# The start of a Mamba and mixture-of-experts kernel: the first chunk in halves, with a queue of its own for the B and C rows

## The chip, the cores and the metric

The kernel runs on one core of one Trainium2 chip. The metric is the device time of one execution in microseconds; the time of a kernel is the median over its runs. Data are 32-bit floats. A core has TensorE (matrix products into PSUM), VectorE, ScalarE, GpSimd, and SP, which only issues transfers. ScalarE and GpSimd can issue transfers too.

## The reference, cut to what matters

The input x has 4 batches of 1024 tokens with 128 channels. Layer 0 is a selective state-space mixer (256 inner channels, 16 states) times the SiLU of a mixture of 8 experts; layer 1 is a linear attention times another mixture of experts. The change is in the front of layer 0's mixer:

```python
xn = layernorm(x)
xs, z = split(xn @ W_in)
xc = silu(causal_conv4(xs) + conv_b)
dbl = xc @ W_x                       # 64 columns for dt, 16 for B, 16 for C
dt = softplus(dbl[..., :64] @ W_dt + b_dt)
A = -exp(A_log)
h_t = exp(dt * A) * h_(t-1) + (dt * xc) * B_t      # a scan over t, for each of 16 states
y_t = sum over states of h_t * C_t
```

## The kernel before, in words

Channels lie on the 128 partitions, in two halves (`DK` = 2), tokens along the free axis. The sequence is cut into chunks of 512 tokens (`HALF`, eight chunks, `q`), so a batch has two. For each chunk and each of the 16 states there is one scan step, 144 in all, since the last chunk is done in two pieces. A step has: two decays on ScalarE (`pA`, L939), the product `dBx` = dtx times the B row on GpSimd (L738), two scans on VectorE (L1305), the product with the C row (`hc`, L1313), and eight transposes that sum over the states on TensorE (L829).

`make_plan` writes one list of stages, and each engine walks that list and takes its own part. So the order on each engine is fixed, and semaphores tie the engines together. The list begins with the front of chunk 0, one stage after the other: `xload`, `norm`, `xn`, `xT`, `xs`, `conv`, `thc`, `xc`, `dbl`, `dtr`, `soft`, `ln`, `dt`, `decay`. The scan steps follow, and between them stand the fronts of later chunks, the routing, the expert tiles and the sums ("extras").

The stages of the front, by lines of the kernel before. At the start VectorE clears `gy` (a tile of zeros), all PSUM banks, `xs`, `bd` and `bdw`, then waits for all small loads (`mix_loaded`), halves the convolution's weights `cw` and `cb`, and negates `am` after ScalarE has taken its Exp (L1146 to L1157). `norm`: mean and variance of eight tiles of 128 tokens on VectorE (L1167, L1170), eps and the power -1/2 on GpSimd (L681, L683). `xn`: eight normalising operations (L1182). `xT`, twice: four transposes (L765) and a copy (L963). `xs`, once per channel half: one projection (L804) and two ScalarE operations that read it, a copy (L1022) and the last tap of the convolution (L1024). `conv`: three taps per half on VectorE (L1267). `thc` and `xc`: SiLU as a Tanh (L1030) and one VectorE operation (L1277). `dbl`: the product with `W_x` (L810) and a copy (L1036). `dtr`: the product with `W_dt` (L817) and bias (L1048). `soft`, `ln`, `dt`: softplus as max(v, 0) + ln(1 + exp(-|v|)) with a correction of the rounding of 1 + e; Abs, Exp and Ln on ScalarE (L1053, L1055, L1059), then four VectorE operations (L1284 to L1287), and `dtx` = dt times xc (L1291).

The B and C rows of `dbl` go to device memory (`bc_rows`, L598, on SP's queue), and from there one row of B and one of C per step is spread over all partitions (`bcb`, three buffers, L951, on ScalarE's queue). At the start SP issues, in this order: x, the small loads (L584), six stores of zeros into the routed rows (L591), the weights of the experts (`exp_loads`, L594), six more stores of zeros, the store of the B and C rows, and the second batch of x (L581). The zeros are needed by the first scatter of tokens (L696), the experts' weights by their scaling on VectorE (L1329 to L1331), which stands behind the first scan step.

## Time and profile before

| | |
|---|---|
| time, median of 3 runs | 1222.59 us (1222.11 to 1223.76) |
| time of the profiled execution | 1228.98 us |
| its span | 1227.1 us |
| TensorE matmul busy | 919.4 us, 75% |
| VectorE busy | 967.1 us, 79% |
| ScalarE busy | 610.6 us, 50% |
| GpSimd busy | 594.1 us, 48% |
| mean granted TensorE clock | 0.874 of 2.4 GHz |

The span is the time from the first to the last event of the core in the profiled execution. Busy times are those in which the engine worked; they overlap one another. The page cuts the span into 40 equal slices of 30.7 us and gives each a digit. The timeline lists instructions in order of time; "x4" means that four are merged into a row, whose duration is then that of the group. What stands in brackets is the idle time before it and what ended it.

### The profile page before, as it was taken

To read this page: it belongs to the slowest core of one execution; us is meant where nothing else is said; L and a number is where in the kernel's file an instruction comes from. 1 tells how busy PE (TensorE), PEld (TensorE's weight loads), DVE (VectorE), ACT (ScalarE), POOL (GpSimd) and SP (SyncE) were. 2 spreads that over 40 slices of the span, in tenths; PEclk is the share of its full clock that TensorE was granted. 3 is DMA by queue.
4 is the path that set the end of the run, shared out by engine and by line. 5 is a ranking of instruction groups with operands and counts; after the bars stand their busy time and mean duration, and the time that the engine had idled before them with its cause. 6 is when DMAs were issued, how large, how long until landed. Compare 5 with 4: busy or idle time off the path is not lost.

```text
span 1227.1 us, 16938 instructions
## 1 busy us (share of the span) xinstructions
PE 919.4 (75%) x4540; PEld 650.9 (53%) x4540; DVE 967.1 (79%) x1808; ACT 610.6 (50%) x1585; POOL 594.1 (48%) x420
## 2 busy tenths in 40 slices
PE   2277587877677778876887889778676788889678
PEld 0054366545455555555655566556454565566456
DVE  4298689987998988877988797969658886888455
ACT  1343554563556545653665465645445554655233
POOL 0036523767436633785336333784774646335500
PEclk9676798896899988898998899988878897989888
DMA  8924334455434434553544534355644356445201
GB/s 263 284 73 105 101 86 98 136 141 140 120 104 112 110 85 108 141 139 117 121 95 115 123 97 112 108 159 133 152 115 113 79 117 167 103 110 133 66 5 31
DMA packets 168650, 144.71 MB, mean 118 GB/s; under 512 B 15680, under 2 KB 135536, under 8 KB 168560
## 3 DMA queue, kind: packets, MB, share of 16 engines
q10 hardware_dynamic: 39168, 67.12, 24.0%
q1 hardware_dynamic: 121712, 60.78, 17.4%
q0 software_dynamic: 7680, 15.74, 4.0%
q8 instruction: 41, 0.67, 0.2%
q14 instruction: 49, 0.40, 0.1%
HBM read 106.88 MB, written 36.70 MB: 117 GB/s over the span
## 4 chain that ended last, share of the span: by engine, by line
PE 30%; DVE 28%; issue 15%; POOL 11%; ACT 7%; SPq 4%; DMA 3%; another core or an unknown queue 1%; ACTq 1%; DVEq 0%; POOLq 0%
DVE pA L1305 10%; PE pM L919 5%; POOL dBx L738 5%; PE pH L829 3%; PE pM L909 3%; DVE hj L1341 3%; POOL rows_in L696 3%; PE p L884 3%; POOL gy L712 3%; PE pG L881 2%; PE pU L882 2%; SPq L594 2%; DVE hj L1353 2%; PE pG L884 1%; PE pH L897 1%
## 5 line engine op out<-in xcount | busy, mean ns | idle before, releaser
L738 POOL TENSOR_TENSOR dBx<-dtx,bcb 128x1024 f32<-128x1024 f32 (+1 forms) x144 | 305.7, 2123 | 453.7 <-DVE pA L1305 405.0
L829 PE MATMUL pH<-const,hc 128*128 128x128 f32 x1024 | 165.9, 310 | 55.2 <-DVE hc L1313 49.3
L1305 DVE TENSOR_TENSOR_SCAN pA<-pA,carry,dBx 128x512 f32<-128x512 f32 (+1 forms) x160 | 162.9, 1064 | 43.8 <-ACT pA L939 22.5
L939 ACT ACTIVATE pA<-dt,am 128x512 f32<-128x512 f32 (+1 forms) x288 | 173.9, 639 | 27.4 <-DVE hc L1313 19.0
L1305 DVE TENSOR_TENSOR_SCAN pA<-pA,dBx 128x512 f32<-128x512 f32 x128 | 149.8, 1216 | 38.7 <-POOL dBx L738 25.3
L829 PEld LDWEIGHTS pH<-const,hc 128*128 128x128 f32 x1024 | 131.2, 159 | 76.5 <-DVE hc L1313 57.4
L909 PE MATMUL pM<-const,hj 128*128 128x128 f32 (+3 forms) x636 | 131.5, 304 | 46.5 <-ACT hT L1114 13.3
L1313 DVE TENSOR_TENSOR hc<-pA,bcb 128x1024 f32<-128x1024 f32 (+1 forms) x144 | 159.3, 1106 | 5.0
L696 POOL DMA_INDIRECT rows_in<-xn,slots x120 | 127.4, 1062 | 30.4 <-issue 27.5
L909 PEld LDWEIGHTS pM<-const,hj 128*128 128x128 f32 (+3 forms) x636 | 74.2, 142 | 120.5 <-issue 82.2
L1111 ACT ACTIVATE yj<-pM 128x128 f32<-128x128 f32 x236 | 65.3, 277 | 137.7 <-PE pM L919 117.6
L1114 ACT ACTIVATE hT<-pM 128x256 f32<-128x256 f32 (+1 forms) x272 | 113.5, 417 | 34.8 <-PE pM L909 32.3
L881 PE MATMUL pG<-w13a,xgT 128*128 x184 | 84.1, 542 | 48.8 <-DVE hj L1353 46.7
L712 POOL DMA_INDIRECT gy<-rows_out,slots x96 | 94.9, 989 | 27.7 <-issue 24.4
L1341 DVE SCALAR_TENSOR_TENSOR hj<-tj,pG 128x352 f32<-128x352 f32 (+2 forms) x153 | 68.1, 445 | 47.0 <-ACT tj L1101 23.7
L919 PE MATMUL pM<-w2b,hT 128*128 (+1 forms) x448 | 99.4, 323 | 2.3 <-ACT hT L1114 1.5
L919 PEld LDWEIGHTS pM<-w2b,hT 128*128 128x128 f32 x448 | 73.6, 206 | 23.7 <-issue 8.0
L919 PE MATMUL pM<-w2a,hT 128*128 x552 | 81.5, 286 | 0.0
L882 PE MATMUL pU<-w13a,xgT 128*128 x184 | 79.3, 516 | 0.0
L919 PEld LDWEIGHTS pM<-w2a,hT 128*128 128x128 f32 x552 | 74.3, 204 | 0.2
L884 PE MATMUL p<-w13b,xgT 128*128 x108 | 50.6, 553 | 29.8 <-issue 15.2
L881 PEld LDWEIGHTS pG<-w13a,xgT 128*128 128x128 f32 x184 | 31.1, 207 | 69.0 <-issue 68.4
(205 smaller groups left out, 1536.2 us busy)
## 6 DMA issues: line engine op xcount, KB each, us to landing
bcb<-bc_rows ACTq DMA_DIRECT2D x112, 512.0 KB
rows_out<-yj SPq DMA_DIRECT2D x236, 64.0 KB
xg<-rows_in SPq DMA_DIRECT2D x176, 64.0 KB
bcb<-bc_rows ACTq DMA_DIRECT2D x32, 256.0 KB
rows_in<-gy SPq DMA_DIRECT2D x8, 512.0 KB, 5.6
mixed<-s_st SPq DMA_DIRECT2D x12, 256.0 KB, 2.4
so<-rows_out SPq DMA_DIRECT2D x6, 512.0 KB
sr<-mixed SPq DMA_DIRECT2D x6, 512.0 KB
```

The lines of the kernel that those rows point to most:

```text
L696: pool.indirect_dma_start(rows_in[l][b % 2], bass.IndirectOffsetOnAxis(ap=slots[l][b][:, c, k:k + 1], axis=0), xn[:, c, :], None).then_inc ...
L712: pool.indirect_dma_start(gy3[:, k, c, :] if b == LAST else gy[:, k, c, :], None, rows_out[l][b], bass.IndirectOffsetOnAxis(ap=slots[l][b] ...
L738: pool.tensor_tensor(dBx[:, N % 2, :, 0:t1 - t0], dtx[q % 2][:, :, t0:t1], row, ALU.mult).then_inc(dBx_ready, 1)
L829: last = mm(pH[:, half, c * DI + k * P:c * DI + (k + 1) * P], hc[:, N % 2, k, t * P:(t + 1) * P], ident, is_transpose=True, start=(n == 0 ...
L881: mm(pG[:, 0:hid], tok, w[:, 0:hid], start=True, stop=True).then_inc(gate_full, 1)
L909: last = pe.transpose(pM[0:w, m * P:(m + 1) * P], hj[i][:, k % 2, m * P:m * P + w], ident)
L919: last = mm(pM[:, YA:YA + P], hT[i][0:wd, m * P:(m + 1) * P], w[0:wd, m, :], start=(m == 0), stop=(m == len(ks) - 1))
L939: A(pA[:, k, 0:t1 - t0], dt[q % 2][:, k, t0:t1], ACT.Exp, scale=am[:, k, n:n + 1]).then_inc(decay_ready, 1)
L1114: last = A(hT[i][:, 0:w], pM[:, 0:w], ACT.Copy)
L1305: dve.tensor_tensor_scan(pA[:, k, 0:w], pA[:, k, 0:w], dBx[:, N % 2, k, 0:w], carry[:, k, N % NS:N % NS + 1] if N in carry_after else 0.0, ...
L1313: dve.tensor_tensor(hc[:, N % 2, :, 0:w], pA[:, :, 0:w], row, ALU.mult).then_inc(hc_ready, 1)
L1341: dve.scalar_tensor_tensor(out=hj[i][:, k % 2, 0:hid], in0=tj_of(i, k), scalar=1.0, in1=gate_bank(i, k)[:, 0:hid], op0=ALU.add, op1=ALU.mu ...
```

## The change

The list of stages of chunk 0 is new, and so is what they hold:

- The norm of batch 0 is done in halves of four tiles. Only the first half stands ahead of the projections; the second stands behind `xc`, and its transposes behind `dt`. Eps is now added on VectorE, for every front. GpSimd keeps the power, with its own tile of -1/2.
- VectorE clears one PSUM bank (`pM`) at the start and no other. The tile of zeros, `bd` and `bdw` are cleared on GpSimd.
- The waits are split: TensorE waits for `const` and `w_in`, VectorE for `cw` and `cb`, and all for the other small loads only at `dbl`, where the Exp of `am` now stands. `const`, `cw` and `cb` are loaded on ScalarE's queue.
- SP issues x, `w_in`, the other small loads, the experts' weights, and then all twelve stores of zeros.
- The convolution of a half follows its own projection; Tanh and, for chunk 0, `xc` are done by halves, and the product with `W_x` waits for each half by itself.
- For chunk 0 the store of the B and C rows is issued by ScalarE right behind the copy of `dbl`, and the first load of them behind Exp.
- Softplus: three VectorE operations stand at the stage `ln` and wait for Exp only; behind the logarithm one addition is left. This holds for all chunks.

```diff
@@ -217,9 +217,8 @@
-    plan = [("xload", 0), ("norm", 0, 0), ("xn", 0, 0), ("xT", 0, 0, 0), ("xs", 0, 0), ("xT", 0, 0, 1), ("xs", 0, 1),
-            ("conv", 0, 0), ("conv", 0, 1), ("thc", 0), ("xc", 0), ("dbl", 0), ("dtr", 0, 0), ("dtr", 0, 1),
-            ("soft", 0), ("ln", 0), ("dt", 0)]
+    plan = [("xload", 0), ("norm", 0, 0), ("xT", 0, 0, 0), ("xs", 0, 0), ("xs", 0, 1), ("conv", 0, 0), ("conv", 0, 1), ("thc", 0),
+            ("xc", 0), ("xn", 0, 0), ("dbl", 0), ("dtr", 0, 0), ("dtr", 0, 1), ("soft", 0), ("ln", 0), ("dt", 0), ("xT", 0, 0, 1)]
...
@@ -537,17 +538,21 @@
...
-            (const[:], T["const"]),
-            (w_in[:], T["L0_attn_W_in"]),
...
-            (cw[:], T["L0_attn_conv_w"].rearrange("(k p) j -> p k j", p=P)),
-            (cb[:], T["conv_b"]), (bdt[:], T["b_dt"]), (dpar[:], T["D_param"]),
...
+            (bdt[:], T["b_dt"]), (dpar[:], T["D_param"]),
...
@@ -580,8 +585,11 @@
+                        sp.dma_start(w_in[:], T["L0_attn_W_in"]).then_inc(w_in_loaded, 16)
...
+                        for dst, src in exp_loads:
+                            sp.dma_start(dst, src).then_inc(exp_loaded, 16)
...
-                            if l == 0:
-                                for dst, src in exp_loads:
-                                    sp.dma_start(dst, src).then_inc(exp_loaded, 16)
-                elif kind == "dbl":
+                elif kind == "dbl" and a[0]:
...
@@ -669,18 +674,23 @@
...
-                if kind == "norm":
+                if kind == "xload" and a[0] == 0:
+                    pool.memset(mhalf[:], -0.5).then_inc(mhalf_ready, 1)
+                    pool.memset(gy[:, 0], 0.0).then_inc(zero_tile, 1)
+                    pool.memset(bd[:], 0.0)
+                    pool.memset(bdw[:], 0.0).then_inc(zero_tile, 1)
+                elif kind == "norm" or (kind, *a) == ("xn", 0, 0):
...
-                        pool.wait_ge(mix_loaded, 16 * len(mix_loads))
...
-                    pool.wait_ge(stats_ready, F)
+                        c0, c1 = ((0, HT), (HT, CT))[kind == "xn"]
+                    no = F + (F > 1 or kind == "xn")
...
+                    pool.wait_ge(stats_ready, no)
...
-                    pool.tensor_scalar(vpe[:, cs], mv[:, cs, 1], EPS, None, ALU.add).then_inc(ve_ready, 1)
-                    pool.wait_ge(ve_ready, F)
-                    pool.tensor_tensor(rstd[:, cs], vpe[:, cs], mhalf[:, cs], ALU.pow).then_inc(rstd_ready, 1)
+                    pool.tensor_tensor(rstd[:, c0:c1], vpe[:, c0:c1], mhalf[:, c0:c1], ALU.pow).then_inc(rstd_ready, 1)
...
@@ -754,11 +764,15 @@
                 if kind == "xload" and a[0] == 0:
-                    pe.wait_ge(mix_loaded, 16 * len(mix_loads))
-                    pe.wait_ge(prepared, 1)
+                    pe.wait_ge(const_loaded, 16)
+                    pe.wait_ge(w_in_loaded, 16)
+                    pe.wait_ge(psum_cleared, 1)
                 elif kind == "xT":
...
-                    pe.wait_ge(xn_ready, front_no[l, b])
+                    if (l, b, m) == (0, 0, 0):
+                        pe.wait_ge(xn_first, 1)
+                    else:
+                        pe.wait_ge(xn_ready, front_no[l, b])
...
                 elif kind == "dbl":
...
-                    pe.wait_ge(xc_ready, q + 1)
+                    if q == 0:
+                        pe.wait_ge(mix_loaded, 16 * len(mix_loads))
...
+                        pe.wait_ge(xc_ready, DK * q + k + 1)
...
                 elif kind == "xs":
...
+                    act.wait_ge(conv_scaled, 1)
...
@@ -1024,16 +1039,23 @@
                 elif kind == "thc":
...
-                    act.wait_ge(conv_ready, 2 * (q + 1))
...
-                    A(v[:], ca[:], ACT.Tanh).then_inc(thc_ready, 1)
+                    for k in range(DK):
+                        act.wait_ge(conv_ready, DK * q + k + 1)
+                        A(v[:, k, :], ca[:, k, :], ACT.Tanh).then_inc(thc_ready, 1)
                 elif kind == "dbl":
...
+                    if q == 0:
+                        act.wait_ge(mix_loaded, 16 * len(mix_loads))
+                        A(am[:], am[:], ACT.Exp).then_inc(decay_exp, 1)
...
+                    if q == 0:
+                        act.wait_ge(bank_read, use["dbl", q])
+                        act.dma_start(bc_rows[0], dbl[R:R + 2 * NS, :]).then_inc(rows_stored, 16)
...
+                    if q == 0:
+                        bc_load(0)
...
                 elif kind == "decay":
-                    for N in range(BCR):
+                    for N in range(1, BCR):
...
-                    act.wait_ge(prepared, 2)
+                    act.wait_ge(decay_negated, 1)
...
@@ -1143,44 +1167,56 @@
...
-            dve.memset(gy[:, 0], 0.0).then_inc(zero_tile, 1)
-            for t in (pA, pH, pG, pU, p1, pM):
-                dve.memset(t[:], 0.0)
-            dve.memset(xs[:], 0.0)
-            dve.memset(bd[:], 0.0)
-            dve.memset(bdw[:], 0.0).then_inc(prepared, 1)
-            dve.wait_ge(mix_loaded, 16 * len(mix_loads))
-            dve.tensor_scalar(cw[:], cw[:], 0.5, None, ALU.mult)
-            dve.tensor_scalar(cb[:], cb[:], 0.5, None, ALU.mult)
-            dve.wait_ge(decay_exp, 1)
-            dve.tensor_scalar(am[:], am[:], -1.0, None, ALU.mult).then_inc(prepared, 1)
-            dve.wait_ge(prepared, 2)
+            def moments(src, c0, c1):
...
+                for c in range(c0, c1):
+                    last = dve.bn_stats(stats[:, c, :], src[:, c, :])
+                link(last)
+                for c in range(c0, c1):
+                    last = dve.bn_aggr(mv[:, c, :], stats[:, c, :])
+                link(last)
+                dve.tensor_scalar(vpe[:, c0:c1], mv[:, c0:c1, 1], EPS, None, ALU.add).then_inc(stats_ready, 1)
...
+            def normalise(src, c0, c1):
+                for c in range(c0, c1):
+                    last = dve.tensor_scalar(xn[:, c, :], src[:, c, :], mv[:, c, 0:1], rstd[:, c:c + 1], ALU.subtract, ALU.mult)
+                return last
...
+            dve.memset(pM[:], 0.0).then_inc(psum_cleared, 1)
...
                 if kind == "norm":
...
+                    if (l, b) == (0, 0):
+                        moments(src, 0, HT)
+                        dve.wait_ge(stats_ready, 1)
+                        dve.wait_ge(rstd_ready, 1)
+                        normalise(src, 0, HT).then_inc(xn_first, 1)
+                        dve.wait_ge(conv_loaded, 32)
+                        dve.tensor_scalar(cw[:], cw[:], 0.5, None, ALU.mult)
+                        dve.tensor_scalar(cb[:], cb[:], 0.5, None, ALU.mult).then_inc(conv_scaled, 1)
+                        dve.wait_ge(conv_scaled, 1)
+                    else:
+                        moments(src, *cols(l, b))
...
-                    dve.wait_ge(stats_ready, F)
-                    dve.wait_ge(rstd_ready, F)
...
+                    if (l, b) == (0, 0):
+                        moments(src, HT, CT)
+                        dve.wait_ge(stats_ready, 2)
+                        dve.wait_ge(rstd_ready, 2)
+                        normalise(src, HT, CT).then_inc(xn_ready, 1)
+                    else:
+                        dve.wait_ge(stats_ready, F + 1)
+                        dve.wait_ge(rstd_ready, F + 1)
+                        normalise(src, *cols(l, b)).then_inc(xn_ready, 1)
...
                 elif kind == "conv":
...
-                    dve.wait_ge(bank_read, use["xs", q, 1])
+                    dve.wait_ge(bank_read, use["xs", q, k])
...
                 elif kind == "xc":
...
-                    dve.wait_ge(thc_ready, q + 1)
...
-                    dve.scalar_tensor_tensor(out=xc[q % 2][:], in0=v[:], scalar=1.0, in1=ca[:], op0=ALU.add, op1=ALU.mult
-                                             ).then_inc(xc_ready, 1)
-                elif kind == "dt":
+                    if q:
+                        dve.wait_ge(thc_ready, DK * (q + 1))
+                        dve.scalar_tensor_tensor(out=xc[q % 2][:], in0=v[:], scalar=1.0, in1=ca[:], op0=ALU.add, op1=ALU.mult
+                                                 ).then_inc(xc_ready, DK)
+                    else:
+                        for k in range(DK):
+                            dve.wait_ge(thc_ready, k + 1)
+                            dve.scalar_tensor_tensor(out=xc[0][:, k, :], in0=v[:, k, :], scalar=1.0, in1=ca[:, k, :], op0=ALU.add, op1=ALU.mult
+                                                     ).then_inc(xc_ready, 1)
+                elif kind == "ln":
...
+                    if q == 0:
+                        dve.wait_ge(decay_exp, 1)
+                        dve.tensor_scalar(am[:], am[:], -1.0, None, ALU.mult).then_inc(decay_negated, 1)
...
-                    dve.wait_ge(ln_ready, q + 1)
+                    dve.wait_ge(act_chain, 2 * q + 2)
...
-                    link(dve.tensor_tensor(g, dt[q % 2][:], g, ALU.subtract))
-                    dve.scalar_tensor_tensor(out=dt[q % 2][:], in0=v[:], scalar=0.0, in1=g, op0=ALU.max, op1=ALU.add
-                                             ).then_inc(dt_ready, 1)
+                    link(dve.scalar_tensor_tensor(out=g, in0=v[:], scalar=0.0, in1=g, op0=ALU.max, op1=ALU.subtract))
+                elif kind == "dt":
...
+                    dve.wait_ge(ln_ready, q + 1)
+                    dve.tensor_tensor(dt[q % 2][:], dt[q % 2][:], xs[:, :, 0:HALF], ALU.add).then_inc(dt_ready, 1)
...
-                    dve.wait_ge(xc_ready, q + 1)
+                    dve.wait_ge(xc_ready, DK * (q + 1))
...
```

## Rows read from the trace of the kernel before

**Rows 1.** The page: clock and DMA share in 40 slices; shares of the chain by engine.
```profile
PEclk9676798896899988898998899988878897989888
DMA  8924334455434434553544534355644356445201
...
PE 30%; DVE 28%; issue 15%; POOL 11%; ACT 7%; SPq 4%; DMA 3%; another core or an unknown queue 1%; ACTq 1%; DVEq 0%; POOLq 0%
```

**Rows 2.** The chain, 0 to 90 us: start us, duration us, engine and line.
```profile
48.29 4.90 DMA bc_rows<-dbl
53.21 5.64 DMA bcb<-bc_rows
...
58.98 2.35 POOL dBx L738
61.35 2.36 DVE pA L1305 x2
```

**Rows 3.** Timeline of SP's queue: start us, duration us, then what is issued.
```profile
0.73 0.43 SPq L581 DMA_DIRECT2D x<-in_L_attn_x  x1
...
15.79 3.11 SPq L594 DMA_DIRECT2D w13s<-in_L_ffn_sw  x2
...
40.43 7.82 SPq L591 DMA_DIRECT2D rows_in<-gy  x6
...
48.29 1.56 SPq L598 DMA_DIRECT2D bc_rows<-dbl  x1
```

**Rows 4.** Timeline of the compute engines, from the norm to dbl.
```profile
9.83 0.17 DVE L1153 TENSOR_SCALAR cw<-cw 128x8 f32<-128x8 f32 x1 [2.15 <-DMA queryT<-in_queryT]
...
10.31 1.65 DVE L1167 BATCH_NORM_STATS2 stats<-x 128x6 f32<-128x128 f32 x8
...
13.15 1.68 POOL L683 TENSOR_TENSOR rstd<-vpe,const 128x8 f32<-128x8 f32 x1
14.93 2.14 DVE L1182 TENSOR_SCALAR xn<-x,mv,rstd 128x128 f32<-128x128 f32 x8 [2.30 <-POOL rstd L683]
...
17.22 1.09 PE L765 MATMUL pM<-const,xn 128*128 128x128 f32 x4 [17.22 <-DVE xn L1182]
...
19.06 2.08 PE L804 MATMUL pM<-xnT,w_in 128*128 128x512 f32 x2 [0.75 <-ACT xnT L963]
...
21.73 0.77 ACT L1024 ACTIVATE ca<-pM,cb,cw 128x512 f32<-128x512 f32 x1
...
24.42 2.07 PE L804 MATMUL pM<-xnT,w_in 128*128 128x512 f32 x2 [0.69 <-ACT xnT L963]
...
27.88 4.57 DVE L1267 SCALAR_TENSOR_TENSOR ca<-xs,cw,ca 128x512 f32<-128x512 f32 x6 [10.79 <-ACT ca L1024]
...
34.85 3.58 PE L810 MATMUL pM<-xc,w_x 128*96 128x512 f32 x4 [8.36 <-DVE xc L1277]
...
38.47 0.59 ACT L1036 ACTIVATE dbl<-pM 96x512 f32<-96x512 f32 x1 [4.93 <-PE pM L810]
```

**Rows 5.** Timeline of the compute engines, softplus.
```profile
45.74 1.28 ACT L1059 ACT_TABLE_LOAD   x1
...
48.12 0.69 DVE L1284 TENSOR_SCALAR xs<-ca 128x1024 f32<-128x1024 f32 x1 [13.32 <-ACT dt L1059]
...
52.62 1.22 DVE L1291 TENSOR_TENSOR dtx<-dt,xc 128x1024 f32<-128x1024 f32 x1
```

**Rows 6.** DMA issues of 0 to 80 us: KB each, median us to landing.
```profile
w2a<-in_L_ffn_w SPq DMA_DIRECT2D x2, 512.0 KB, 11.0
...
const<-in_const SPq DMA_DIRECT2D x1, 275.5 KB, 4.2
```

**Rows 7.** Line L683 in 900 to 1000 us: duration ns, starts, form.
```profile
L683 POOL TENSOR_TENSOR rstd<-vpe,const x1: 1050/1050/1050, 990.5 to 990.5; 128x4 f32<-128x4 f32 x1
```

**Rows 8.** Timeline of GpSimd from 100 us: the first scatter.
```profile
101.66 1.46 POOL L696 DMA_INDIRECT rows_in<-xn,slots  x1 [0.19 <-issue]
```

**Rows 9.** Busy time per engine, clock and DMA share, one stretch.
```profile
292.00:408.00 116.00, 85.65 (x448) 62.88 (x449) 104.16 (x176) 63.66 (x144) 58.82 (x34) 0.90 0.43 117
```

More of the change, by code:

```diff
@@ L364, in program @@
         queryT = sb("queryT", [P, P])
-        NCONST = 3 * P + NE + NE * CT + TILES + NE + NE * CT
+        NCONST = 3 * P + NE + NE * CT + TILES + NE * CT
         const = sb("const", [P, NCONST])
@@ L372, in program @@
         last_at = 3 * P + NE + NE * CT + TILES
-        mhalf = const[:, last_at:last_at + NE]
-        goes_on = const[:, last_at + NE:NCONST]
+        goes_on = const[:, last_at:NCONST]
         x = sb("x", [P, CT, P])
@@ L389, in program @@
         vpe = sb("vpe", [P, CT])
+        mhalf = sb("mhalf", [P, CT])
         rstd = sb("rstd", [P, CT])
@@ L538, in program, with bc_row @@
         out_rows = [[sem(f"out_rows{i}{s}") for s in range(YR)] for i in range(2)]
+        def bc_row(N):
+            q, t0, t1 = SEGS[N // NS]
+            n = N % NS
+            src = bc_rows[q].rearrange("(w n) t -> n w t", w=2)[n:n + 1, :, t0:t1]
+            return bcb[:, N % BCR, :, 0:t1 - t0], src.broadcast_to([P, 2, t1 - t0])
         block = ctx.enter_context(nc.Block())
         mix_loads = [
-            (const[:], T["const"]),
-            (w_in[:], T["L0_attn_W_in"]),
             (w_x[:], T["L0_attn_W_x"].rearrange("(k p) n -> p k n", p=P)),
@@ L941, in bc_load @@
             def bc_load(N):
-                q, t0, t1 = SEGS[N // NS]
-                n = N % NS
-                if n == 0:
-                    act.wait_ge(rows_stored, 16 * (q + 1))
+                if N % NS == 0:
+                    act.wait_ge(rows_stored, 16 * (SEGS[N // NS][0] + 1))
                 if N >= BCR:
@@ L949, in bc_load @@
                     act.wait_ge(hc_ready, N - BCR + 1)
-                src = bc_rows[q].rearrange("(w n) t -> n w t", w=2)[n:n + 1, :, t0:t1]
-                act.dma_start(bcb[:, N % BCR, :, 0:t1 - t0], src.broadcast_to([P, 2, t1 - t0])).then_inc(bc_loaded[N % BCR], 16)
+                act.dma_start(*bc_row(N)).then_inc(bc_loaded[N % BCR], 16)
             for kind, *a in plan:
                 if kind == "xload" and a[0] == 0:
-                    act.wait_ge(mix_loaded, 16 * len(mix_loads))
-                    A(am[:], am[:], ACT.Exp).then_inc(decay_exp, 1)
-                    act.wait_ge(prepared, 1)
+                    act.dma_start(const[:], T["const"]).then_inc(const_loaded, 16)
+                    act.dma_start(cw[:], T["L0_attn_conv_w"].rearrange("(k p) j -> p k j", p=P)).then_inc(conv_loaded, 16)
+                    act.dma_start(cb[:], T["conv_b"]).then_inc(conv_loaded, 16)
                 elif kind == "xT":
@@ L977, in _ @@
                     b, = a
+                    act.wait_ge(zero_tile, 2)
                     act.wait_ge(bank_full, use["gram", b])
@@ L1045, in _ @@
                     if k == 0:
-                        act.wait_ge(xc_ready, q + 1)
+                        act.wait_ge(xc_ready, DK * (q + 1))
                     act.wait_ge(bank_full, use["dtr", q, k])
@@ L1161, in _ @@
                     l, b = a
-                    F = front_no[l, b]
                     src = x if l == 0 or b >= LAST else xr
@@ L1165, in _ @@
                         dve.wait_ge(x_in, 16 * (b + 1))
-                    for c in range(*cols(l, b)):
-                        last = dve.bn_stats(stats[:, c, :], src[:, c, :])
-                    link(last)
-                    for c in range(*cols(l, b)):
-                        last = dve.bn_aggr(mv[:, c, :], stats[:, c, :])
-                    last.then_inc(stats_ready, 1)
+                    if (l, b) == (0, 0):
[9 more added lines that the diff above has]
+                        moments(src, *cols(l, b))
                 elif kind == "xn":
@@ L1180, in _ @@
                         dve.wait_ge(scattered[pl][pb % 2], 16 * TOPK * CT * (pb // 2 + 1))
-                    for c in range(*cols(l, b)):
-                        last = dve.tensor_scalar(xn[:, c, :], src[:, c, :], mv[:, c, 0:1], rstd[:, c:c + 1], ALU.subtract, ALU.mult)
-                    last.then_inc(xn_ready, 1)
+                    if (l, b) == (0, 0):
[7 more added lines that the diff above has]
+                        normalise(src, *cols(l, b)).then_inc(xn_ready, 1)
                 elif kind == "top":
@@ L1455 @@
         np.eye(P), np.triu(np.ones((P, P)), 1) - 1, np.ones((P, P)), row * np.arange(NE), row * np.tile(P * np.arange(CT), NE),
-        row * np.arange(TILES), row * np.full(NE, -0.5),
+        row * np.arange(TILES),
         row * np.tile(np.arange(CT) > 0, NE)], axis=1).astype(np.float32))
```

20 lines of the change are left out of this document (12 added, 8 removed).

## The prediction

> **What bounds the kernel now.** I read the page's chain first, then the timeline of the first 72 us engine by engine, then the chain of the same stretch, then the queue's landings. The page's chain is spread over TensorE, VectorE, issue and GpSimd, with no one engine behind it [rows 1]: 144 scan steps in a fixed order. Nothing of that order is changed by this edit except in small ways, so the question is where the first scan starts and whether all that follows moves with it. It starts at 61.35 us [rows 2].
>
> The chain of the start shows why. The first dBx on GpSimd (58.98) waits for the first row pair of B and C; that load waits for the store of the rows, and the store stands at 48.29 in SP's queue, though ScalarE had written dbl at 38.47 + 0.59 = 39.06 [rows 2, 4]. In between SP issues six zeroing stores (7.82 us for six, because the queue is full) and before them the expert weights, from 15.79 to 40.43 [rows 3]. So the store loses 9.2 us to its place. Compute was done earlier too: dtx ends at 52.62 + 1.22 = 53.84, and the dBx could start at 53.95 rather than 58.98 [rows 2, 5]. So removing the queue alone is worth 5.0 us; then the arithmetic chain from x is next.
>
> **The chain after the change, step by step.** Start: x. It is the first load of SP's queue, issued at 0.73 [rows 3]; const, queued behind it and issued at 1.22 (0.49 later), takes 4.2 us to land, so by 5.4 [rows 6]. x is earlier than that and is now alone at the head of its queue, but shares the engines with const on ScalarE's. I take 5.0, between 4.2 and 5.4. Before, the norm began at 10.31, because VectorE cleared all of PSUM and then waited for the last small load [rows 4]. VectorE now has one memset ahead of the norm.
>
> - moments: before, 2.84 us from 10.31 to the pow at 13.15, with eight columns and two GpSimd steps; I put 0.5 of it to hand-overs and halve the rest (1.15); eps is now a VectorE op, 0.17 as the small op on cw, plus 0.2 of hand-over: 1.5 [rows 4]. -> 6.5
> - pow: 1.68 for 8 columns, 1.05 for 4 in the one row of that width [rows 4, 7]. -> 7.55 (by half of 1.68 it would be 0.84)
> - four xn: half of 2.14, with both hand-overs 1.35. -> 8.9
> - transposes to x-projection: 17.22 to 19.06, 1.84. -> 10.75
> - first projection and its two ScalarE copies: 19.06 to 22.50, 3.44. -> 14.2. The transposes of the second half no longer stand between the two projections.
> - second projection: 0.14 of hand-over, then 24.42 to the first convolution at 27.88, 3.46. -> 17.8. The first channel half is convolved meanwhile (three ops, 2.29, from 14.2 to 16.5), hidden behind the second projection.
> - second channel half: three ops, half of 4.57. -> 20.1
> - half Tanh and half xc: the whole took 34.85 - 32.45 = 2.40; half of it with a fixed part is 1.35. -> 21.45
> - second half of dbl: half of 3.58 plus 0.05, then the 0.59 copy. The first half ran before. -> 24.0 [all rows 4]
>
> dbl is thus written at 24.0 instead of 39.06. From there to the end of Exp nothing is changed but ScalarE's issue of the store, which lies beside its wait for TensorE's dtr: the table load behind Exp began at 45.74, 6.68 after dbl, so Exp ends at 30.7 [rows 4, 5]. Then two branches. ScalarE: issue of the first B/C load (0.4), table load and Ln (45.74 to 48.12, 2.38): 33.5. VectorE: negated am 0.2, then the three ops in front of the logarithm. The four of before took 48.12 to 52.62, 4.50; without one of 1.25 that is 3.25: 34.2. One op of 1.25 for dt, 1.25 for dtx: 36.7. dBx starts at 36.8, takes 2.35, and the scan starts at **39.2** [rows 2, 5]. VectorE, not Ln, is the later branch by 0.7, so one operation behind the logarithm instead of four is worth 33.5 + 4.5 = 38.0 (start of dtx in the old order) less 35.45 = 2.5 us, not the whole of three ops.
>
> What ScalarE does between Ln and the first decay: the copy of xT and the first Exp (512 wide, at most 0.77 each, as the copy at 21.73), two DMA issues (0.43 each, as SP's first) and a table load (1.28), from 33.5: 37.2, still ahead of dBx's end by 2.0 [rows 3 to 5]. The second half of the norm (four columns) sits on VectorE between xc (21.5) and Exp (30.7), 9 us for some 4 us of work. These cost nothing; if that gap were gone they would cost 4.
>
> **The B and C rows.** Their store is issued at 24.1. In the trace it took 4.90 us in SP's full queue, and the load 5.64 [rows 2]. With those durations the store lands at 29.0, ahead of Exp's end, and the load (issued 30.8) at 36.4, ahead of dtx by 0.3. That is the thinnest margin of the change. The trace has no row of this pair against a backlog of weights. The nearest above are the weight loads themselves, w2a with 11.0 us [rows 6]; the nearest below are the 4.90 and 5.64. At 11.0 each the store lands at 35.1, and as ScalarE waits for it with the table load, Ln, the xT copy and all decays queued behind that wait, the load is issued at 35.2, lands at 46.2 and the scan starts at 48.7. I take a little over the lower end, since the long rows were queued behind 1.4 MB loads of their own queue and this pair is not: 1 us for it. First scan at 40.2, so **21.1 us** earlier.
>
> The page's DMA row stands at 8 and 9 tenths in the first two slices, 61 us [rows 1]; so the rows share full engines, and I weigh what a rule says. The Trainium skill (Trainium Kernel Development and Optimization, Key Constraints) states that DMAs of the SP, ACT and POOL queues share the same 16 engines and that issuing from several only saves the sequencer's issue time: it speaks against an own queue. By it alone the rows would keep waiting for bytes and the pair would cost as in the 11.0 case. The skill's DMA: Bandwidth & Descriptors (Queues, rings and completion order) says that each engine goes round between the queues packet by packet; by that the pair has a half share at least and the lower end holds. No row here decides between them; SP's 7.82 us for six issues shows only that the issue time itself is large.
>
> **What moves with the first scan.** Expert weights are now issued straight behind the small loads, at 6.5 instead of 15.79; the same 24.6 us [rows 3] put the last issue at 31 and its landing at 36 at the latest. Their scaling on VectorE stands behind the first scan (40 + 3.5), so it waits for nothing. Zeroing follows: it had landed by 53.2 before, when the store behind it had [rows 2], and the three B/C loads of 1.5 MB now run among it, so 55 to 58. Its only user, the first scatter on GpSimd, was at 101.66 [rows 8], 80.5 after the shift: 22 us to spare. The second load of x stays behind the zeroing and is wanted by the norm of scan step 10. The PSUM banks that are no longer cleared and the memsets on GpSimd, which has nothing else to do before the first pow, cost nothing. No other time of the start is tied to the clock on the wall, so I count the shift in full.
>
> **Later chunks.** Tanh in halves adds some 0.15 us of ScalarE, 7 times; eps adds a VectorE op of 0.17 and a hand-over in 9 fronts, about 2.5 us if all of it lay on the chain, and takes one GpSimd op from each. The softplus ops of a chunk stand in two scan steps instead of one, with the same op count. I put the sum at 0, between -2 and +2.5.
>
> **Sum.** The profiled execution has a span of 1227.1 and a time of 1228.98; with 21.1 less, a span of 1206.0. The median of the three runs is 1222.59, 6.4 below the profiled one. 1222.6 - 21.1 = **1201.5 us**. Ends of the main case: first scan at 38.4 (x at 4.2, the pair as before) and -2: 1197.6; first scan at 43 and +2.5: 1206.7.
>
> **Rivals.**
> 1. Main case, 1197 to 1208: 0.80.
> 2. The B/C pair is slowed by the weights (toward 11.0 each), ScalarE is held. First scan at 45 to 49: 1207 to 1211. For it: the engines are full. Against it: the pair is small beside them. 0.08. The Key Constraints rule of the Trainium skill named above would give this time.
> 3. The own queue gets nothing until SP's backlog is gone: store at 53, Ln and load behind it, first scan at 60 to 62. That is 1221 to 1223, the case in which the change doesn't do what it says. 0.03. Its mild form, only the queue's 5.0 us won and the arithmetic as late as before, gives 1217.6: 0.02.
> 4. Slower: TensorE's clock. The page's clock row reads low in slices 2 to 5 [rows 1]; a stretch of 116 us at 0.90 has 85.65 us of matmul [rows 9], which at the 1.2 GHz level would be 154, so 38 us more for 116. If the new rhythm of the start kept the clock at 1.2 GHz for 65 us longer, the gain of 21 would be gone; at 80 us the time is 1201.5 + 26.2 = 1227.7. Against it: order and density of the scan stage are the same. 0.04.
> 5. Better than 1197: the clock rises earlier, the projections (2.08 and 2.07 [rows 4]) shorten. 0.03.
>
> **How the numbers follow.** A measurement of this kernel can tell 0.2% (2.4 us) from no change. Faster: cases 1, 2, 5 and the mild 3, 0.93. Within: case 3, 0.03. Slower: case 4, 0.04. The range takes case 1 and the near part of 2: 1196 to 1209.
>
> **What would show it.** dbl's copy should end near 24, Exp near 30.7, the first dBx start near 37 released by VectorE's dtx (if a bcb DMA releases it, the pair is the later); the idle time before Ln shows whether the store held ScalarE; the first scan near 40; the first scatter near 81 and not waiting for the zeroing. From first scan to the end it should take 1165.7 us as before, within 3. The forecast is wrong if x lands later than 6, if pow of four columns costs 1.68, or if that last distance grows.

## The result, and the profile after

The changed kernel took 1193.0 us (median of four runs, 1188.3 to 1197.5) against 1222.4 before; the ratio is 0.9757, with a 95% interval of 0.9716 to 0.9798. That is 29 us less, where 21 were forecast, and outside the forecast range. The profiled execution has a span of 1186.5 us and a time of 1188.29.

The chain of the start, after the change (start us, duration us, engine and line):

```profile
0.72 4.96 DMA x<-in_L_attn_x
...
7.35 1.04 POOL rstd L693
8.50 1.13 DVE xn L1182 x4
...
11.53 2.09 PE pM L818 x2
...
18.54 0.76 DVE ca L1303
...
21.61 3.50 PE pM L826 x4
25.13 0.60 ACT dbl L1055
...
36.99 1.24 DVE dtx L1338
...
38.30 2.35 POOL dBx L748
40.67 2.36 DVE pA L1352 x2
```

SP has left the chain: before, it stood in it from x to the store of the rows [rows 2, 3]. The first scan starts at 40.67 instead of 61.35, 20.7 us earlier; 21.1 were forecast. The queues and what waits for them, from the timeline:

```profile
25.76 0.34 ACTq L1058 DMA_DIRECT2D bc_rows<-dbl  x1
...
28.25 25.81 SPq L599 DMA_DIRECT2D rows_in<-gy  x12
...
31.39 1.06 ACT L1077 ACTIVATE ca<-ca 128x1024 f32<-128x1024 f32 x1
31.40 0.39 ACTq L964 DMA_DIRECT2D bcb<-bc_rows  x1
...
38.30 2.34 POOL L748 TENSOR_TENSOR dBx<-dtx,bcb 128x1024 f32<-128x1024 f32 x1 [13.55 <-DVE dtx L1338]
```

The load of B and C rows is issued at 31.40, as soon as Exp has started, so the store had landed: ScalarE was not held. The dBx was released by dtx on VectorE, not by a transfer; in three other traces it was the transfer (experiment 3). GpSimd's first scatter comes 20.0 us earlier than before [rows 8], straight behind its own work, with no wait for the zeros:

```profile
81.69 1.44 POOL L706 DMA_INDIRECT rows_in<-xn,slots  x1 [0.18 <-issue]
```

So the first scan is where it was forecast, and the missing 8 us lie behind it: from the first scan to the end it took 1145.8 us, where the forecast wanted 1165.7 within 3. I measure the scan stage from the start of the first product with a C row to that of the last (143 steps): 1075.4 us before (63.7 to 1139.1), 1056.6 after. The profiled execution of before is itself 6.6 us over its median, and the one after 4.7 us under it, so these two traces overstate the difference. By the medians the gain is 29.4 us; less these 20.7, some 8.7 us lie behind the first scan. That is why the cause was looked for in groups of traces, below.

One place where the scan stage is shorter shows in VectorE's timeline. The changed kernel, softplus of chunk 5, from scan step 75 to step 77:

```profile
623.97 1.22 DVE L1360 TENSOR_TENSOR hc<-pA,bcb 128x1024 f32<-128x1024 f32 x1
625.12 0.75 DVE L1328 TENSOR_SCALAR xs<-ca 128x1024 f32<-128x1024 f32 x1
625.90 1.23 DVE L1329 SCALAR_TENSOR_TENSOR xs<-xs,ca 128x1024 f32<-128x1024 f32 x1
627.16 1.22 DVE L1330 SCALAR_TENSOR_TENSOR xs<-v,xs 128x1024 f32<-128x1024 f32 x1
...
631.66 1.23 DVE L1360 TENSOR_TENSOR hc<-pA,bcb 128x1024 f32<-128x1024 f32 x1
...
635.06 1.22 DVE L1335 TENSOR_TENSOR dt<-dt,xs 128x1024 f32<-128x1024 f32 x1
636.31 1.23 DVE L1338 TENSOR_TENSOR dtx<-dt,xc 128x1024 f32<-128x1024 f32 x1
...
640.48 1.23 DVE L1360 TENSOR_TENSOR hc<-pA,bcb 128x1024 f32<-128x1024 f32 x1
```

And the same two steps in the kernel of experiment 1 that has the old softplus behind the new front; by chance its step 75 starts at the same time:

```profile
623.97 1.23 DVE L1379 TENSOR_TENSOR hc<-pA,bcb 128x1024 f32<-128x1024 f32 x1
626.09 0.33 ACT L1131 ACTIVATE tj<-pG 128x192 f32<-128x192 f32 x1
626.45 0.35 DVE L1407 SCALAR_TENSOR_TENSOR hj<-tj,pG 128x192 f32<-128x192 f32 x1 [1.25 <-issue]
...
629.07 2.35 DVE L1371 TENSOR_TENSOR_SCAN pA<-pA,dBx 128x512 f32<-128x512 f32 x2 [1.88 <-ACT pA L957]
631.45 1.22 DVE L1379 TENSOR_TENSOR hc<-pA,bcb 128x1024 f32<-128x1024 f32 x1
...
634.85 0.88 DVE L1348 TENSOR_SCALAR xs<-ca 128x1024 f32<-128x1024 f32 x1
...
639.55 1.23 DVE L1357 TENSOR_TENSOR dtx<-dt,xc 128x1024 f32<-128x1024 f32 x1
...
643.72 1.23 DVE L1379 TENSOR_TENSOR hc<-pA,bcb 128x1024 f32<-128x1024 f32 x1
```

Old order: VectorE idles 1.25 + 1.88 = 3.1 us in the first step, while it waits for ScalarE: first, by the times, for `tj` of an expert tile (ready at 626.42), then for the decays. It then has four softplus operations and dtx in one lump of 5.9 us (634.85 to 640.78) in the second. New order: the three operations that need only Exp fill the idle time of the first step. It ends only 0.2 us later (631.66 against 631.45), and the second is 8.8 us long instead of 12.3. The operation count is the same. How much of that a chunk keeps depends on its other steps, as the table below shows.

### The profile page after: what moved, and what is told of

It reads as the page before. It is cut to its first block, busy times and chain, and to the rows that moved or that the text cites. A ratio compares the mean times of both kernels' runs of the same rounds, so it can differ in the third digit from the quotient of the medians.

```text
span 1186.5 us, 16957 instructions
## 1 busy us (share of the span) xinstructions
PE 902.7 (76%) x4540; PEld 640.1 (54%) x4540; DVE 965.7 (81%) x1811; ACT 612.4 (52%) x1593; POOL 594.9 (50%) x415
## 4 chain that ended last, share of the span: by engine, by line
DVE 32%; PE 28%; POOL 15%; issue 12%; ACT 7%; DMA 4%; ACTq 1%; SPq 0%; DVEq 0%; POOLq 0%
DVE pA L1352 11%; POOL dBx L748 6%; POOL gy L722 5%; PE pM L935 4%; DVE hj L1388 3%; PE pH L845 3%; POOL rows_in L706 3%; PE pM L925 3%; PE pG L897 2%; PE p L900 2%; PE pU L898 2%; DVE hj L1400 2%; DVE hc L1360 2%; PE pH L913 1%; PE pG L900 1%
## 5 line engine op out<-in xcount | busy, mean ns | idle before, releaser
L845 PE MATMUL pH<-const,hc 128*128 128x128 f32 x1024 | 162.3, 306 | 49.0 <-DVE hc L1360 45.0
L845 PEld LDWEIGHTS pH<-const,hc 128*128 128x128 f32 x1024 | 128.4, 157 | 68.5 <-DVE hc L1360 52.0
L925 PE MATMUL pM<-const,hj 128*128 128x128 f32 (+3 forms) x636 | 130.2, 302 | 44.5 <-DVE hj L1400 18.3
L706 POOL DMA_INDIRECT rows_in<-xn,slots x120 | 129.8, 1082 | 30.4 <-issue 27.4
L900 PE MATMUL p<-w13b,xgT 128*128 x108 | 48.7, 535 | 30.7 <-DVE hj L1400 30.0
## 6 DMA issues: line engine op xcount, KB each, us to landing
rows_in<-gy SPq DMA_DIRECT2D x8, 512.0 KB, 10.3
```

The costliest lines, as they stand in the source:

```text
L706: pool.indirect_dma_start(rows_in[l][b % 2], bass.IndirectOffsetOnAxis(ap=slots[l][b][:, c, k:k + 1], axis=0), xn[:, c, :], None).then_inc ...
L845: last = mm(pH[:, half, c * DI + k * P:c * DI + (k + 1) * P], hc[:, N % 2, k, t * P:(t + 1) * P], ident, is_transpose=True, start=(n == 0 ...
L925: last = pe.transpose(pM[0:w, m * P:(m + 1) * P], hj[i][:, k % 2, m * P:m * P + w], ident)
```

## The experiments

Times are given as the ratio to the kernel before, run on the same chip in the same group, with its 95% interval. On the chips of experiment 1 and of the last run the kernel before itself scattered from 1220 to 1244 us, so there the traces say more than the times.

**Experiment 1: the front alone, and the softplus alone.** The yardstick, unaltered:

> The changed kernel once more, unaltered, as the yardstick of this group. Its first scan stands at 40.7 us, 20.7 earlier than before, as forecast; its median was 29.4 us below the one before and its runs lay 9 us apart. If the scatter belongs to the kernel, the median comes out between 1189 and 1197 again and the runs lie 6 us or more apart. If the 29.4 was chance of that chip, it comes out near 1201.

Measured: 0.9777 [0.9715, 0.9838]. The median was 1204.2, above the 1189 to 1197 expected, on a chip where before had 1232.6; the ratio agrees with the first measurement. The scan stage was 1064.5 us long.

The front alone: eps, Tanh and softplus of later chunks as before.

```diff
+                        pool.tensor_scalar(vpe[:, c0:c1], mv[:, c0:c1, 1], EPS, None, ALU.add).then_inc(ve_ready, 1)
...
+                    if q:
+                        act.wait_ge(conv_ready, DK * (q + 1))
+                        A(v[:], ca[:], ACT.Tanh).then_inc(thc_ready, DK)
+                        continue
...
+                    if q:
+                        continue
...
+                    if q:
+                        link(dve.tensor_scalar(g, ca[:], 1.0, None, ALU.add))
+                        link(dve.scalar_tensor_tensor(out=g, in0=g, scalar=1.0, in1=ca[:], op0=ALU.subtract, op1=ALU.subtract))
+                        link(dve.tensor_tensor(g, dt[q % 2][:], g, ALU.subtract))
+                        dve.scalar_tensor_tensor(out=dt[q % 2][:], in0=v[:], scalar=0.0, in1=g, op0=ALU.max, op1=ALU.add
+                                                 ).then_inc(dt_ready, 1)
```

> The changed front of chunk 0, with all that acts in later chunks undone: softplus in the old order, Tanh in one piece and eps on GpSimd for every chunk and batch but the first. Theory S (the 8 us beyond the forecast come from what the change does to later chunks): 1201.5, all of 21 us and no more. Theory T (an earlier start alone changes the rhythm of the scan stage, and with it TensorE's clock and the waits): 1193, the same as the whole change.

Measured: 0.9845 [0.9785, 0.9905], 19 us of 1222, with the first scan at 41.23. Theory S had said 1201.5, a ratio of 0.983; theory T 0.976, outside the interval. The scan stage is 1071.2 us long, hardly shorter than before.

The softplus alone, on the kernel before:

```diff
-                elif kind == "dt":
+                elif kind == "ln":
                     q, = a
                     g = xs[:, :, 0:HALF]
-                    dve.wait_ge(ln_ready, q + 1)
+                    dve.wait_ge(act_chain, 2 * q + 2)
...
-                    link(dve.tensor_tensor(g, dt[q % 2][:], g, ALU.subtract))
-                    dve.scalar_tensor_tensor(out=dt[q % 2][:], in0=v[:], scalar=0.0, in1=g, op0=ALU.max, op1=ALU.add
-                                             ).then_inc(dt_ready, 1)
+                    link(dve.scalar_tensor_tensor(out=g, in0=v[:], scalar=0.0, in1=g, op0=ALU.max, op1=ALU.subtract))
+                elif kind == "dt":
+                    q, = a
+                    dve.wait_ge(ln_ready, q + 1)
+                    dve.tensor_tensor(dt[q % 2][:], dt[q % 2][:], xs[:, :, 0:HALF], ALU.add).then_inc(dt_ready, 1)
```

> The kernel before, with only the softplus split: three VectorE operations at the stage ln, one behind the logarithm, for all chunks. In the traces of before and after, the pair of scan steps that holds these stages gained 2.6, 0.1, 3.0, 1.1 and 1.3 us in five of the seven chunks. Theory S: 1222.4 less 6 to 9, so 1214 to 1216. Theory T: 1222 to 1223.

Measured: 0.9897 [0.9836, 0.9957], 12.6 us less, with the first scan at 60.64, only 0.7 earlier than before. That is more than theory S asked for (0.993 to 0.995, inside the interval) and speaks against T (1.000, outside). 0.9845 x 0.9897 = 0.974: front and softplus add up to the whole change (0.976).

**Experiment 2: undoing the split, delaying the start, and the queue both ways.**

> The changed kernel with softplus in the old order from the second chunk on; eps on VectorE and Tanh in halves stay. If the split of softplus is the cause of the gain in later chunks: the scan steps 10 to 14 of chunks 3, 5, 6 and 7 are again 1 to 3 us longer each, and the time is that of the run with the front alone, 0.984 to 0.985 of before. If eps or Tanh is the cause: it stays near 0.977.

The softplus part of the diff of the front alone, and no other:

```diff
+                    if q:
+                        continue
                     g = xs[:, :, 0:HALF]
                     dve.wait_ge(act_chain, 2 * q + 2)
...
+                        link(dve.tensor_tensor(g, dt[q % 2][:], g, ALU.subtract))
```

Measured: 0.9889 [0.9855, 0.9923]; 0.984 to 0.985 was expected. Step 76 takes 12.3 us again, as before (8.8 with the split). The stretches with the softplus of chunks 3, 5, 6 and 7 are 0.7, 2.9, 0.9 and 4.1 us longer than in the first trace of the changed kernel. Not every long step is a loss: in chunk 4's stretch step 60 takes 15.5 us again instead of 10.6, but the step before it takes 6.0 instead of 7.9 and the two behind it 17.0 instead of 20.0, so the whole stretch changes by less than 0.1. The scan stage is 1071.1 us long, as with the front alone: the gain of the later chunks is gone with the split. The time is 5 us over the front alone, and the intervals overlap.

> The whole change, with VectorE held back by 20 chained memsets of an unused buffer behind the arrival of x, some 20 us, so that the first scan stands near 61 us as before. Theory S (front and later chunks add): 1222.4 - 8 = 1214, ratio 0.993 to 0.994. Theory T (an earlier start alone brings the later gain): 1222, ratio 1.000.

```diff
             dve.memset(pM[:], 0.0).then_inc(psum_cleared, 1)
+            dve.wait_ge(x_in, 16)
+            for _ in range(20):
+                link(dve.memset(xc[1][:], 0.0))
```

Measured: 0.9942 [0.9915, 0.9970]. The first scan came at 64.00, 2.7 us later than before, and still the time is 7.1 us less (theory S: 0.993 to 0.994). So the later gain needs no early start: theory T is out.

> The kernel before, with only this changed for chunk 0: ScalarE issues the store of the B and C rows behind the copy of dbl (near 39.1 us), and the first load of them behind Exp (near 45). By the sum of the forecast dtx is then next: first dBx at 53.95 instead of 58.98, first scan 5.0 us earlier at 56.3, time 1217.4. If weights and zeros in the other queue slow the pair to 11 us each, the first load lands at 61 or later and nothing is won.

```diff
-                elif kind == "dbl":
+                elif kind == "dbl" and a[0]:
...
+                    if q == 0:
+                        act.wait_ge(bank_read, use["dbl", q])
+                        act.dma_start(bc_rows[0], dbl[R:R + 2 * NS, :]).then_inc(rows_stored, 16)
...
+                    if q == 0:
+                        bc_load(0)
...
-                    for N in range(BCR):
+                    for N in range(1, BCR):
```

Measured: 0.9964 [0.9946, 0.9982]. The timeline of its start:

```profile
39.66 0.35 ACTq L1039 DMA_DIRECT2D bc_rows<-dbl  x1
...
39.77 2.04 PE L817 MATMUL pM<-dbl,w_dt 64*128 64x512 f32 x2 [0.77 <-ACT dbl L1036]
...
42.65 2.07 PE L817 MATMUL pM<-dbl,w_dt 64*128 64x512 f32 x2 [0.84 <-ACT v L1051]
...
55.83 2.34 POOL L738 TENSOR_TENSOR dBx<-dtx,bcb 128x1024 f32<-128x1024 f32 x1 [40.59 <-DVE dtx L1296]
```

The first dBx is at 55.83, released by dtx as forecast, and not at 53.95: 3.2 us instead of 5.0. The two dtr products took 2.04 and 2.07 us here, where the kernel before had 1.09 and 1.68, which is 1.3 us of the 1.9; dbl was written at 39.62 instead of 39.06, which is the rest. The time, 4.4 us less, agrees with the 5 forecast.

> The changed kernel without its own queue: the store of the B and C rows stands on SP behind all twelve stores of zeros, and the loads at the first decay, as before. The rest of the change stays. SP's issue ends near 48 us as before, the store lands near 52.6, the load near 58.3, the first scan stands near 60.7. So of the 20.7 us of the front none but 0.6 is left, and the time is 1222.4 - 0.6 - 8 for the later chunks = 1214. If the arithmetic and not the queue was the bound, 1193 to 1200.

```diff
-                elif kind == "dbl" and a[0]:
+                elif kind == "dbl":
...
-                    if q == 0:
-                        act.wait_ge(bank_read, use["dbl", q])
-                        act.dma_start(bc_rows[0], dbl[R:R + 2 * NS, :]).then_inc(rows_stored, 16)
...
-                    if q == 0:
-                        bc_load(0)
...
-                    for N in range(1, BCR):
+                    for N in range(BCR):
```

Measured: 0.9875 [0.9849, 0.9901]. The end of its chain to the first scan:

```profile
44.76 1.82 SPq L599
46.63 5.03 DMA bc_rows<-dbl
51.68 5.69 DMA bcb<-bc_rows
...
57.50 2.35 POOL dBx L748
59.87 2.36 DVE pA L1347 x2
```

dbl was ready at 26.0, and the first scan is at 59.87, 1.5 us ahead of before [rows 2]. Without the own queue the 13.1 us that the arithmetic gained at dbl are worth 1.5. Without the faster arithmetic the queue is worth 3.2. Together they are worth 20.7. The front half of the expectation held (60.7); its time did not (1214 against 1207), for the scan stage was 1051.3 us long, the shortest of all.

**Experiment 3: what is left of eps and Tanh, and a finer split.**

> The changed kernel again, as the yardstick of this group: 0.976 to 0.978 of before.

Measured: 0.9753 [0.9731, 0.9776]. This trace has its first scan at 42.75 us, 2.1 later than the first trace of the same kernel, and the load of the B and C rows is what the first dBx waited for:

```profile
32.73 7.52 DMA bcb<-bc_rows
...
38.31 1.23 DVE L1338 TENSOR_TENSOR dtx<-dt,xc 128x1024 f32<-128x1024 f32 x1
...
40.38 2.34 POOL L748 TENSOR_TENSOR dBx<-dtx,bcb 128x1024 f32<-128x1024 f32 x1 [15.79 <-DMA bcb<-bc_rows]
```

The load took 7.52 us among the stores of zeros, against 5.64 before [rows 2], and landed 0.7 us after dtx was ready. The same load took 7.11 us with the front alone and 7.78 in the next run, and was the last there too. The other 1.3 us are the `dtr` products again, 2.04 and 2.07 us.

> The changed kernel with eps on GpSimd and Tanh in one piece from the second batch and chunk on; the split of softplus stays for all chunks. The earlier groups leave two readings. If eps and Tanh cost 4 to 6 us in later chunks (front alone 0.9845 against 0.9889 with both, softplus old in each): 0.972 to 0.974. If that difference was scatter: the same as the changed kernel, 0.976 to 0.978.

```diff
+                    if q:
...
+                        A(v[:], ca[:], ACT.Tanh).then_inc(thc_ready, DK)
...
+                        pool.tensor_scalar(vpe[:, c0:c1], mv[:, c0:c1, 1], EPS, None, ALU.add).then_inc(ve_ready, 1)
```

Measured: 0.9725 [0.9701, 0.9749]. 3.4 us less by the ratio, 0.8 by the medians, and the intervals overlap. This stays open; the two comparisons put the cost of eps and Tanh at 3.4 us here and 5 us in experiment 2, neither clear of noise, and neither shows a gain.

> The changed kernel with softplus spread further from the second chunk on: the first two correction operations one scan step earlier (two, one and two operations in three steps instead of three and two). If it is the lump on VectorE that costs, another 1 us a chunk is won in the chunks where the step with three operations is VectorE's, in all 2 to 6 us, ratio 0.972 to 0.975. If the steps in which the operations now stand were full already: no change.

```diff
+        at(s + 8, "corr", q)
         at(s + 9, "ln", q)
...
+                    if q == 0 or kind == "corr":
+                        dve.wait_ge(act_chain, 2 * q + 2)
+                        link(dve.tensor_scalar(g, ca[:], 1.0, None, ALU.add))
```

Measured: 0.9797 [0.9774, 0.9819], 5.4 us slower than the changed kernel in the same group; the intervals all but part. The stretches of scan steps that hold the softplus of chunks 4 and 6 took 62.2 and 62.6 us instead of 60.0 and 60.4: their step 10 (counted from the chunk's first) grew from 10.1 and 9.9 to 12.0 and 11.8, and step 13 from 8.8 to 11.2. Step 10 was not full: in chunk 3's step 58 VectorE idled 1.49 us in the changed kernel and 1.37 here. But the idle time ends as Exp does:

```profile
476.83 0.23 DVE L1273 TENSOR_TENSOR over<-rk,const 128x64 f32<-128x64 f32 x1 [1.49 <-ACT rk L988]
...
477.05 0.69 DVE L1330 TENSOR_SCALAR xs<-ca 128x1024 f32<-128x1024 f32 x1 [1.37 <-ACT ca L1078]
```

The first row is of the changed kernel, the second of this run. The two moved operations need Exp, so they could not use the idle time before it, and all that stands behind them in VectorE's list moved back by some 1.9 us. Step 13 is longer by GpSimd: VectorE waits 4.63 us for `dBx` in step 61 instead of 2.19, because GpSimd issues five transfers ahead of it in that step instead of three.

> Both of the last two together. If both gains are real and add: 0.968 to 0.972. If neither is: 0.976 to 0.978.

Its diff is those of the last two runs, without eps and Tanh and with the finer split, together.

Measured: 0.9788 [0.9754, 0.9823], as slow as the spread alone.

**The last run: the old order where the split had cost time.**

> The changed kernel with softplus in the old order for the second chunk alone, and eps and Tanh as in the run with these two undone. In the traces the split cost 2.5 us in the second chunk (scan steps 9 to 15: 59.6 us with it, 57.1 without), because VectorE's eight normalising operations stand in the step that gets the three softplus operations. If that reading holds: steps 9 to 15 take 57.1 again, and the time is 2.5 us under that run, ratio 0.970 to 0.971 against its 0.9725. If the 2.5 us come back later: 0.9725 again.

```diff
+                    if q == 1:
+                        continue
                     g = xs[:, :, 0:HALF]
...
+                    if q == 1:
+                        link(dve.tensor_scalar(g, ca[:], 1.0, None, ALU.add))
+                        link(dve.scalar_tensor_tensor(out=g, in0=g, scalar=1.0, in1=ca[:], op0=ALU.subtract, op1=ALU.subtract))
+                        link(dve.tensor_tensor(g, dt[q % 2][:], g, ALU.subtract))
...
```

Eps and Tanh are undone as in the run without them.

Measured: 0.9757 [0.9670, 0.9844], no verdict, and not the 0.970 to 0.971 expected. Steps 9 to 15 took 57.3 us, as the reading said. Up to step 96 the scan stage was 744.8 us long, the shortest of all traces (the changed kernel: 747.5, 748.8 and 752.3). Then steps 104 to 107 took 53.1 instead of 43.4, with TensorE at a mean clock of 0.79; such stretches come in the changed kernel too, below.

**All traces side by side.** Mean length, in us, of scan steps 9 to 15 of each chunk (the stretch with the softplus of the next one), by the starts of the products with the C row. Four traces have the old order in later chunks (before, the front alone, the split undone, the queue only), seven the split as in the changed kernel:

| softplus of chunk | 1 | 2 | 3 | 4 | 5 | 6 | 7 | sum |
|---|---|---|---|---|---|---|---|---|
| old order | 57.1 | 47.7 | 48.7 | 60.4 | 51.6 | 61.2 | 66.4 | 393.1 |
| split in two | 59.6 | 46.2 | 47.9 | 60.0 | 48.2 | 60.4 | 63.5 | 385.8 |
| split in three | 58.7 | 47.0 | 47.4 | 62.2 | 47.8 | 62.6 | 62.4 | 388.1 |

The whole scan stage: 1071.4 us on average in the old order (1067.9 to 1075.4), 1058.3 with the split (1051.3 to 1068.8), 1062.9 with the split in three. Of the 13.1 us, 7.3 lie in the softplus stretches. The other 5.8 do not lie where an instruction was moved. They are mostly behind step 104, and there single executions differ by as much. By the medians only 1.4 us (8.7 less 7.3) are left beyond the softplus stretches. Step 104 and steps 104 to 107 in the changed kernel, first as run in experiment 3 (columns as in [rows 9]):

```profile
862.66:873.68 11.02, 9.62 (x46) 6.31 (x44) 5.09 (x10) 6.01 (x21) 9.02 (x8) 0.86 0.47 108
...
862.66:906.09 43.43, 29.75 (x142) 19.93 (x140) 35.93 (x85) 24.82 (x66) 27.90 (x22) 0.89 0.55 123
```

And as run in experiment 1:

```profile
858.93:874.80 15.87, 13.52 (x48) 8.68 (x47) 5.59 (x9) 4.93 (x17) 12.67 (x12) 0.61 0.40 102
...
858.93:910.92 51.99, 39.71 (x166) 25.83 (x164) 33.88 (x84) 25.16 (x68) 27.50 (x22) 0.76 0.47 114
```

The kernel is the same and VectorE's busy time no longer, 35.9 and 33.9 us, but the four steps took 8.6 us more. 4.9 of them lie in step 104, where the clock explains the busy time: TensorE had 0.61 instead of 0.86, was busy 13.5 us instead of 9.6 with about as many products (48 and 46), and 9.62 x 0.86 / 0.61 is 13.6. The rows of four steps can't be compared in this way, since one has 24 products more (166 and 142) that the other execution had already done. Over all traces the mean clock alone does not order the lengths: the split undone has 0.77 in these steps and took 42.8 us. So the clock is shown for step 104 of this pair; for the rest it is not.

## Why the prediction was wrong

The failed step is the sum of the paragraph on later chunks: "I put the sum at 0, between -2 and +2.5". I had compared operation counts, and a moved operation of equal length was worth nothing by that. What counts is the step in which it stands. In the old order VectorE had up to 3.1 us idle in one step and a lump of 5.9 us in the next, and a scan step is not ready for the next one until VectorE is through. Shown by the runs: 7.3 us in the softplus stretches (table), gone when the split is undone, there when only the split is made. With 21.1 + 7.3 the forecast would have been 1194.2, within 1.2 us of the result. My range allowed 2 us for this term; it was 7.3 in the stretches, 8.7 by the medians and 13.1 by the mean of the traces.

Point by point for the front:

- The queue as bound and the arithmetic behind it: right, and shown by the queue alone and the queue undone. That neither is worth much alone (3.2 and 1.5 us) followed from the same sum.
- Arrival of x: forecast 5.0, measured 0.72 + 4.96 = 5.68. A miss of 0.7, inside what I called wrong only beyond 6.
- Pow of four columns: forecast 1.05, measured 1.03.
- First half of the `dbl` product beside the second half's work: wrong. The order on VectorE is convolution 0, convolution 1, then xc 0, xc 1, so the first half of xc started behind the second convolution. The four products ran as one block, 3.50 us from 21.61, where I had counted 1.8. dbl was written at 25.73 instead of 24.0. I had read the waits and not the order of VectorE's own list.
- The B and C pair: the store landed 5.0 us after its issue (4.90 before [rows 2]) among the weights. The load was slowed, by 1.5 to 2.1 us in the three traces that show it (7.11 to 7.78 us against 5.64), so the 1 us that I added for contention was of the right kind. In the first trace it cost nothing, because dtx itself was 1.5 us late. So 40.67 against 40.2 is partly luck: the misses of 0.7 and 1.0 us at x and dbl took the place of the 1 us at the load. Over the traces with the new front, the queue and no delay the first scan lies between 40.30 and 43.39.
- Zeroing: its twelve stores took 25.81 us to issue, some 2.2 each, and with 10.3 us to land the last was there near 64, where I had said 55 to 58; the scatter at 81.69 did not wait.
- No shift lost: right, the first scatter moved by 20.0 us.

The time fell where I had put rival 5, better than 1197 at a chance of 0.03, but not by its mechanism: the projections took 2.07 us each, as before. The rival that TensorE's clock eats the gain did not come. But steps 104 to 107 differ by up to 9 us between executions of kernels with the same split, with the clock as the cause in the one step where it could be worked out, and my range had no share for such scatter on the fast side. Whether the 5.8 us beyond the softplus stretches come from the split by way of the clock, or by chance of which executions were profiled, these runs don't settle.

## What to carry to other kernels

Cost a moved operation by the idle time of its engine in the step it leaves and in the step it enters, not by its length. Print both steps of the timeline and add up the idle brackets, but only those that end after the operation's own inputs are ready: the finer split put 1.9 us into a step with 1.5 us idle and lost all of it, because Exp came at the end of that idle time. Two bounds that end within a few us of each other (here a queue and a chain of arithmetic) are worth almost nothing one at a time and all of it together. And before a transfer or product is counted as overlapped by halves, follow the order of every engine that makes the halves, not only the waits.

## What the runs showed of the hardware

The small store on ScalarE's queue was not slowed by a full SP queue: 5.0 us to land against 4.90 in SP's queue, while w2a's loads took 10.6 us there. The 512 KB load behind it was slowed by the stores of zeros: 7.11, 7.52 and 7.78 us where it can be read, against 5.64. The Trainium skill (DMA: Bandwidth & Descriptors, Queues, rings and completion order) says the engines go round between queues; both agree with that. Its other rule is that several issuing engines only save issue time (Trainium Kernel Development and Optimization, Key Constraints). The runs agree with it by the letter: once issued, the store took 5.0 us in either queue. But the issue time was the large part, for with the store in SP's queue twelve stores of zeros took 18.3 us to issue ahead of it. In the prediction, in the second rival too, I had read the rule as if the bytes themselves had to wait.

The price was paid by SP's queue: its stores of zeros took 8.1 to 10.3 us to land in the nine traces with the new front at its own time and the own queue, against 5.6 before and 6.1 without it, and 25.81 us to issue instead of 18.3.
